# Gated cross-attention and FFN on one core: queries projected from an x turned on the host, with the layer norm folded into the weights and the rotation tables

## The chip, the cores and the metric

The kernel runs on one core of one Trainium2 chip. The metric is device microseconds of one execution. Every time in this document comes from such an execution or from its hardware trace.

## The reference

Sixteen batches of 256 tokens with 512 channels attend to 16 contexts of 256 tokens with 256 channels (32 heads of 16), and an FFN follows. Cut to what matters here:

```
def _layernorm(x, axis=-1, eps=1e-05):
    m = jnp.mean(x, axis=axis, keepdims=True)
    v = jnp.var(x, axis=axis, keepdims=True)
    return (x - m) / jnp.sqrt(v + eps)
...
q = (x @ Wq).reshape(b, n, N_HEADS, HEAD_DIM)
k, v = jnp.split(ctx @ Wkv, 2, axis=-1)
...
q = apply_axial_rope(q, pos_map)
k = apply_axial_rope(k, ctx_pos_map)
logits = jnp.einsum('bqhd,bkhd->bhqk', q, k) * scale
w = jax.nn.softmax(logits, axis=-1)
attn = jnp.einsum('bhqk,bkhd->bqhd', w, v)
...
x = x + jnp.tanh(g_xattn[0]) * _L0_xattn_ref(_layernorm(x), ctx_1024, pos, pos, Wq, Wkv, Wout, bout)
x = x + jnp.tanh(g_ffn[0]) * _L0_ffn_ref(_layernorm(x), gate_w, up_w, down_w, expert_weight, ln_gamma, ln_beta)
```

The rotation turns pairs of query and of key channels by angles that depend on the token's position: out = x1·cos − x2·sin and x1·sin + x2·cos.

## The kernel before

Each engine runs its own instruction stream, written out by hand; semaphores join them. The attention half is a software pipeline. Iteration i has 16 steps (s = 0 to 15), one for each pair of heads. In each step TensorE (PE) does first `logits_a` of one batch (stk and stq into the PSUM tile pA), then `logits_b` of another (into pB), then in some steps `times_v` (probabilities times values into pO, one group of four heads at a time), and last the jobs that the table `SCHEDULE` names for the step: K0, K1, Q0, Q1 project a tile of 128 tokens; kT0 to qT1 turn rotated tiles; V, O and m are values, output projection and the maxima turned; b0 and b1 spread the softmax denominators. X0 and X1 turn a normalised tile of x, so that Q0 and Q1 can take it as their stationary operand. `LAG` says how many batches ahead of i a job works: two for all of the query and key side, so they run in iterations 0 to 13.

VectorE (DVE) follows in the same steps: `maxima` (pA to mneg), then the evacuation of the jobs of the step before. pA is one tile: `logits_a` of step s+1 waits until `maxima` of step s is done. In step 5 and step 14 DVE also runs `reciprocals`: a RECIPROCAL on den, a CAST to den_hi and a TENSOR_TENSOR to den_lo, each waiting for the last.

The products are done in two float32r parts: a rounded value (hi, by ScalarE or GpSimd) and the rest (lo). For a query tile t of batch b the chain before is:

```
ln_statistics: bn_stats, bn_aggr of xin[t]          DVE
inv_std:       var+eps, then power -0.5 into rstd    POOL
ln_apply:      xn = (xin[t] - mean) * rstd           DVE, 128x512
X:             4 transposes of xn into pP            PE
evacuate X:    xnT[0] = round(pP)                    ACT, 128x512
               xnT[1] = pP - xnT[0]                  DVE, 128x512
Q:             12 products of xnT and wq_s           PE
evacuate Q:    rot_q = pP * cos, rot2 = pP' * sin    DVE, 2 x 128x512
rope_sum:      rot_q += rot2                         POOL
```

GpSimd (POOL) does these in an order of its own in each iteration: `inv_std`, `rope_sum` K0, `rest_av` (waits for ACT's rounding `round_av` of step 4), `rope_sum` Q0, two additions of gbout to xres, `rope_sum` K1, `rest_av`, `rope_sum` Q1, `inv_std`, `split_ctx`. SyncE (SP) issues all DMAs in one in-order queue. ACT takes the exponentials out of pB, evacuates hi parts and copies pO to av_s (`take_av`). Before the pipeline stands an opening (`OPENING`) that prepares batches 0 and 1; after it the FFN runs over eight blocks of 512 tokens. In iteration 15 `norm_in` and `turned` already prepare the first FFN tiles.

## Time and profile before

| | us |
|---|---|
| median of 3 runs (1580.32 to 1586.48) | 1585.53 |
| time of the profiled execution | 1587.19 |
| its span | 1585.4 |
| PE busy | 1522.9 (96%) |
| DVE busy | 982.8 (62%) |
| ACT busy | 632.4 (40%) |
| POOL busy | 337.9 (21%) |

The opening lasts to about 62 us, the attention pipeline to about 745 us, and the rest is the FFN. The span is the time from the first to the last instruction in the trace, the time adds what lies around it (1.8 us). A busy PE is not a PE at its peak, since the ends of pipelined matmuls are modelled. The granted clock, in tenths of full speed, is a row of the page.

### The profile page before, as it was taken

The page shows a single profiled execution, that of the slowest core. Times are in us where ns is not written, and L with a number is a line of the kernel's source. Part 1 is how long each engine was busy: PE and PEld are TensorE (multiplying, and loading weights), DVE is VectorE, ACT ScalarE, POOL GpSimd, SP SyncE. Part 2 cuts the span into 40 slices and gives each one's busy share as a digit, 9 for nine tenths or more (in the row PEclk, how much of TensorE's full clock was granted, in tenths as well). Part 3 has the DMA queues.
Part 4 walks back from the last instruction along what each step waited for, and adds up shares of the span by engine and source line. Part 5 has one row for each costly group of instructions (what it writes and reads, how often), then busy time and mean ns, then how long its engine had stood idle before and what let it go on. Part 6 is the DMA issues. An engine that isn't in the chain of part 4 may idle for free.

```text
span 1585.4 us, 25920 instructions
## 1 busy us (share of the span) xinstructions
PE 1522.9 (96%) x9498; PEld 1127.8 (71%) x9498; DVE 982.8 (62%) x1416; ACT 632.4 (40%) x962; POOL 337.9 (21%) x406
## 2 busy tenths in 40 slices
PE   7789999999999999978999999999999999999997
PEld 6556666666666666545787888878878878788886
DVE  7788888888888888755663535426344364353524
ACT  3265555555556565655442222222222222222221
POOL 5323233233323323211101102102010020110202
PEclk9699999999999999987999999999999999999999
DMA  6645555555565555543430101101010011010101
GB/s 171 141 97 142 132 132 134 129 144 133 130 144 129 126 126 137 121 121 97 140 100 14 47 20 47 34 1 54 27 34 28 20 47 34 14 47 20 54 0 41
DMA packets 80623, 131.11 MB, mean 83 GB/s; under 512 B 21624, under 2 KB 35064, under 8 KB 80504
## 3 DMA queue, kind: packets, MB, share of 16 engines
q1 hardware_dynamic: 80504, 129.48, 31.9%
q8 instruction: 80, 1.31, 0.3%
q14 instruction: 39, 0.32, 0.1%
HBM read 51.17 MB, written 16.78 MB: 43 GB/s over the span
## 4 chain that ended last, share of the span: by engine, by line
PE 84%; DVE 8%; issue 4%; POOL 2%; ACT 1%; DMA 0%; SPq 0%; POOLq 0%; DVEq 0%; ACTq 0%
PE pP L1111 17%; PE pT L1111 11%; PE pA L1312 11%; PE pO L1111 11%; PE pB L1312 11%; PE pO L1237 6%; PE pA L1209 6%; DVE mneg L1532 4%; PE pM L1111 3%; PE pB L1225 3%; PE pP L1118 2%; PE pM L1279 1%; PE pT L1193 1%; PE pM L1118 1%; PE pM L1185 1%
## 5 line engine op out<-in xcount | busy, mean ns | idle before, releaser
L1532 DVE TENSOR_REDUCE mneg<-pA 128x4 f32<-128x1024 f32 x250 | 305.7, 1223 | 111.9 <-PE pA L1209 109.0
L1010 ACT ACTIVATE probs<-pB 128x1024 f32<-128x1024 f32 x249 | 256.1, 1029 | 220.0 <-PE pB L1225 209.9
L1635 DVE TENSOR_TENSOR relu<-relu 128x512 f32<-128x512 f32 x128 | 88.3, 690 | 252.6 <-ACT hid L1064 252.6
L810 POOL TENSOR_SCALAR var_eps<-meanvar 128x1 f32<-128x1 f32 x96 | 34.5, 360 | 965.8 <-DVE meanvar L1414 965.6
L1312 PE MATMUL pA<-dn,hid 128*128 128x512 f32 x768 | 197.1, 392 | 1.7 <-DVE hid L1637 1.5
L1312 PE MATMUL pB<-dn,hid 128*128 128x512 f32 x768 | 195.0, 389 | 0.0
L1111 PE MATMUL pP<-fT,up 128*128 128x512 f32 x768 | 188.5, 394 | 0.0
L1111 PE MATMUL pO<-fT,up 128*128 128x512 f32 x768 | 184.9, 390 | 0.1
L1312 PEld LDWEIGHTS pA<-dn,hid 128*128 128x128 f32 x768 | 142.9, 188 | 34.4 <-DVE hid L1637 5.1
L1111 PEld LDWEIGHTS pO<-fT,up 128*128 128x128 f32 x768 | 143.9, 188 | 30.7 <-issue 0.8
L1312 PEld LDWEIGHTS pB<-dn,hid 128*128 128x128 f32 x768 | 144.2, 188 | 30.0
L1111 PEld LDWEIGHTS pP<-fT,up 128*128 128x128 f32 x768 | 142.0, 188 | 30.1
L1209 PE MATMUL pA<-stk,stq 48*128 48x256 f32 x1000 | 129.4, 338 | 28.0 <-DVE mneg L1532 25.1
L1209 PEld LDWEIGHTS pA<-stk,stq 48*128 48x128 f32 x1000 | 76.8, 190 | 103.7 <-issue 54.0
L1237 PE MATMUL pO<-probs,v 128*17 128x256 f32 x2048 | 138.8, 390 | 2.0 <-ACT probs L1010 2.0
L1057 ACT ACTIVATE relu<-pO 128x512 f32<-128x512 f32 x64 | 38.3, 598 | 241.6 <-PE pO L1111 241.6
L1057 ACT ACTIVATE relu<-pP 128x512 f32<-128x512 f32 x64 | 38.3, 598 | 193.7 <-PE pP L1111 193.7
L1225 PE MATMUL pB<-stq,stk 50*128 50x256 f32 x996 | 102.0, 283 | 0.0
L1111 PE MATMUL pT<-wo,aT_hi 128*128 128x512 f32 x256 | 98.4, 426 | 1.1 <-DVE numer L1470 0.6
L1111 PE MATMUL pT<-ex,fT 128*128 128x512 f32 x384 | 92.3, 389 | 0.0
L1637 DVE TENSOR_TENSOR hid<-relu,hid 128x512 fp32r<-128x512 f32 x128 | 88.7, 693 | 4.4
L1111 PE MATMUL pP<-wq,xnT 128*128 128x512 f32 x336 | 90.7, 405 | 0.0
(200 smaller groups left out, 1997.3 us busy)
## 6 DMA issues: line engine op xcount, KB each, us to landing
stk<-kT SPq DMA_DIRECT2D x180, 128.0 KB, 2.9
stq<-qT SPq DMA_DIRECT2D x180, 128.0 KB, 3.0
fres<-x_scratch SPq DMA_DIRECT2D x34, 256.0 KB, 2.8
xin<-x SPq DMA_DIRECT2D x32, 256.0 KB, 2.9
numer<-av_s SPq DMA_DIRECT2D x128, 64.0 KB, 2.4
xres<-x SPq DMA_DIRECT2D x32, 256.0 KB, 2.8
x_scratch<-xres SPq DMA_DIRECT2D x32, 256.0 KB, 2.1
out<-y_s SPq DMA_DIRECT2D x32, 256.0 KB, 2.0
```

Source lines behind the costliest of these rows:

```text
L810: nc.gpsimd.tensor_scalar_add(var_eps[:], meanvar[:, 1:2], EPS).then_inc(ve_made, 1)
L1010: nc.scalar.activation(probs[:, s % 4, :, :, :].rearrange("p a b s -> p a (b s)"), psum[:, :, :], ACT.Exp).then_inc(exp_done, 1)
L1057: nc.scalar.activation(relu[m % 2][:], pU[m % 2], ACT.Relu).then_inc(relu_made, 1)
L1111: last = nc.tensor.matmul(dst, lhs(a, c), rhs(w, c), start=(c == 0 and (a, w) == PASSES[0]), stop=(c == chunks_ - 1 and (a, w) == PASSES[-1]))
L1118: last = nc.tensor.transpose(dst[:, c * P:(c + 1) * P], src(c), ident[:])
L1209: last = nc.tensor.matmul(psum[:, q, t * S:(t + 1) * S], st_q[par][rows, s, t * P:(t + 1) * P], st_k[par][rows, s, :], start=True, stop=True)
L1225: last = nc.tensor.matmul(psum[:, q, t * S:(t + 1) * S], st_k[par][rows, s, t * P:(t + 1) * P], st_q[par][rows, s, :], start=True, stop=True)
L1237: last = nc.tensor.matmul(pO[32 * j:32 * j + HD + 1, 0:S], v_s[par][:, t, 4 * g + j, :], probs[:, (2 * g + j // 2) % 4, j % 2, t, :], star ...
L1312: last = nc.tensor.matmul(acc[u], hid[m % 2][x_][:, u * P:(u + 1) * P], dn_s[w][:, m, :], start=(m == 0 and k == 0), stop=(m == MC - 1 and ...
L1532: nc.vector.tensor_reduce(mneg[par][:, :, 2 * u:2 * u + 2].rearrange("p t q -> p q t"), psum[:, :, :].rearrange("p q (t k) -> p q t k", t= ...
L1635: nc.vector.tensor_tensor(r[:], r[:], r[:], ALU.mult).then_inc(sq_made, 1)
L1637: nc.vector.tensor_tensor(hid[m % 2][1][:], r[:], hid[m % 2][0][:].bitcast(F32), ALU.subtract).then_inc(hid_lo, 1)
```

## The change

- The host passes x a second time, each 128-token tile turned (`xT`). `load_xT` brings it into the tile xn, and `split_x` on POOL makes xnT[0] and xnT[1] from it, for every batch from 2 on. X0 and X1 leave the schedule, and with them ln_apply and both evacuations in the loop (the opening keeps them for batches 0 and 1).
- The mean is taken out of the weights: in the opening PE multiplies wq by a matrix of 1/512 (eight products into pO), ACT copies the result, SP loads wq's four chunks again into the probs tile, and POOL subtracts and splits them anew (`centre_weights`, twelve instructions of 128x512). ACT waits for two chunks before the first exponential of iteration 0 and for all four in its step 3; PE waits for them before Q0 of batch 2.
- The factor 1/std goes into the tables: `scale_tables` on DVE multiplies the tile's 32 columns of cos_t and of sin_t by rstd, in step 3 for tile 0 and in step 8 for tile 1, after the key's rotation has used them and a step ahead of the query's.
- `times_v` and `take_av` of group 1 move from step 4 to 5, of group 3 from 8 to 9.
- At the pipeline's end `norm_in` stands one step earlier, and POOL's first inv_std for the FFN ahead of rest_av.

```
@@ SCHEDULE
-    0: ("X0",),
+    0: (),
-    5: ("kT0", "X1"),
+    5: ("kT0",),
+VALUES = {2: 0, 5: 1, 6: 2, 9: 3, 10: 4, 12: 5, 14: 6}
@@ planned work at the end
-        norm_at = {(i, s - 1): u for (i, s), u in tile_at.items()}
+        norm_at = {(i, s - 2): u for (i, s), u in tile_at.items()}
@@ SyncE
             def load_x(b, t):
...
-                    sp.wait_ge(xn_made, n - 1)
+                    sp.wait_ge(xn_made if n <= TT * 2 + 1 else st_made, n - 1)
...
+            def load_xT(b, t):
+                if (b, t) == (2, 0):
+                    sp.wait_ge(*done_of("X1", 1))
+                else:
+                    sp.wait_ge(xT_split, 2 * (split_no(b, t) - 1))
+                alone(sp)
+                sp.dma_start(xn[:], xT[b * TT + t]).then_inc(xT_in, INC)
...
+            load_xT(2, 0)
+            sp.wait_ge(*done_of("kT1", 1))
+            sp.wait_ge(w_lo, KC - 2 + CC)
+            for c in range(KC):
+                sp.dma_start(raw_again[c], chunks[CC + c][0]).then_inc(w_again[c], INC)
@@ GpSimd
+            def split_x(b, t):
+                n = split_no(b, t)
+                used, of = ("Q0", b) if t else ("Q1", b - 1)
+                pool.wait_ge(*done_of(used, of))
+                pool.wait_ge(xT_in, INC * n)
+                alone(pool)
+                xv = xn[:].rearrange("p (c s) -> p c s", c=KC)
+                nc.gpsimd.tensor_copy(xnT[0][:], xv).then_inc(xT_split, 1)
+                pool.wait_ge(xT_split, 2 * n - 1)
+                nc.gpsimd.tensor_tensor(xnT[1][:], xv, xnT[0][:].bitcast(F32), ALU.subtract).then_inc(xT_split, 1)
...
                 if prepares:
                     rope_sum(b2, "Q0")
+                    split_x(b2, 1)
@@ ScalarE
-                    if s % 2 == 0 and s and within(i):
-                        take_av(i, s // 2 - 1)
+                    if s in VALUES and within(i):
+                        take_av(i, VALUES[s])
...
+            act.wait_ge(col_done, 1)
+            nc.scalar.copy(col_mean, pO[:, :]).then_inc(col_made, 1)
             later_setup()
@@ TensorE, end of the opening
+                for c in range(KC):
+                    for w in range(2):
+                        last = nc.tensor.matmul(pO[:, :], mean_w[:], wq_s[w][:, c, :],
+                                                start=(c == 0 and w == 0), stop=(c == KC - 1 and w == 1))
@@ VectorE
+            def scale_tables(b, t):
+                n = TT * b + t
+                dve.wait_ge(rstd_made, n + 1)
+                dve.wait_ge(*taken_of(f"K{t}", b))
+                alone(dve)
+                for side in (cos_t, sin_t):
+                    own = side[:, n, :, :, :].rearrange("p w k l -> p (w k l)")
+                    nc.vector.tensor_scalar(own, own, rstds[t][:, 0:1], None, ALU.mult).then_inc(scaled, 1)
...
-                    elif s == 3 and within(i + 2) and not first:
-                        ln_apply(i + 2, 1)
+                    elif s in (3, 8) and within(i + 2) and not first:
+                        scale_tables(i + 2, 0 if s == 3 else 1)
...
-                    elif s == 15 and within(i + 3):
-                        ln_apply(i + 3, 0)
```

On DVE, from step 3 to step 6 of one iteration of the loop, before:

```order
255 L1470 TENSOR_TENSOR numer<-pT,numer 128x512
256 L1418 TENSOR_SCALAR xn<-xin,meanvar,rstd 128x512
257 L1532 TENSOR_REDUCE mneg<-pA 128x2x2
258 L1460 TENSOR_TENSOR low<-pM,low 16x256
259 L1454 TENSOR_TENSOR rot_q<-pP,cos_t 128x512
```

The same place on DVE after the change:

```order
243 L1552 TENSOR_TENSOR numer<-pT,numer 128x512
244 L1607 TENSOR_SCALAR cos_t<-cos_t,rstd 128x32
245 L1607 TENSOR_SCALAR sin_t<-sin_t,rstd 128x32
246 L1623 TENSOR_REDUCE mneg<-pA 128x2x2
247 L1542 TENSOR_TENSOR low<-pM,low 16x256
248 L1536 TENSOR_TENSOR rot_q<-pP,cos_t 128x512
```

One 128x512 instruction on xn became two of 128x32 on the tables; two more stand behind the rotation of K1 in step 8.

On POOL, one iteration before (rot_k and rot_q are the rope sums, the sum over rest is rest_av):

```order
107 L817 TENSOR_TENSOR rot_k<-rot_k,rot 128x512
108 L802 TENSOR_TENSOR rest<-numer,aT_hi 128x512
109 L817 TENSOR_TENSOR rot_q<-rot_q,rot 128x512
110 L849 TENSOR_TENSOR xres<-xres,gbout 128x512 x2
111 L817 TENSOR_TENSOR rot_k<-rot_k,rot 128x512
112 L802 TENSOR_TENSOR rest<-numer,aT_hi 128x512
113 L817 TENSOR_TENSOR rot_q<-rot_q,rot 128x512
```

The same iteration on POOL after the change:

```order
142 L852 TENSOR_TENSOR rot_k<-rot_k,rot 128x512
143 L837 TENSOR_TENSOR rest<-numer,aT_hi 128x512
144 L852 TENSOR_TENSOR rot_q<-rot_q,rot 128x512
145 L861 CAST xnT<-xn 128x512
146 L863 TENSOR_TENSOR xnT<-xn,xnT 128x512
147 L909 TENSOR_TENSOR xres<-xres,gbout 128x512 x2
148 L852 TENSOR_TENSOR rot_k<-rot_k,rot 128x512
149 L837 TENSOR_TENSOR rest<-numer,aT_hi 128x512
150 L852 TENSOR_TENSOR rot_q<-rot_q,rot 128x512
151 L861 CAST xnT<-xn 128x512
152 L863 TENSOR_TENSOR xnT<-xn,xnT 128x512
```

A CAST and a TENSOR_TENSOR of 128x512 follow each of the two query sums.

On PE, steps 4 and 5 and the head of step 6 before:

```order
344 L1209 MATMUL pA<-stk,stq 128x256 x4
345 L1225 MATMUL pB<-stq,stk 128x256 x4
346 L1237 MATMUL pO<-probs,v 17x256 x8
347 L1111 MATMUL pT<-wv,ctx 128x512 x6
348 L1209 MATMUL pA<-stk,stq 128x256 x4
349 L1225 MATMUL pB<-stq,stk 128x256 x4
350 L1118 MATMUL pM<-ident,rot_k 128x128 x4
351 L1118 MATMUL pP<-ident,xn 128x128 x4
352 L1209 MATMUL pA<-stk,stq 128x256 x4
```

The same place on PE after:

```order
336 L1289 MATMUL pA<-stk,stq 128x256 x4
337 L1305 MATMUL pB<-stq,stk 128x256 x4
338 L1181 MATMUL pT<-wv,ctx 128x512 x6
339 L1289 MATMUL pA<-stk,stq 128x256 x4
340 L1305 MATMUL pB<-stq,stk 128x256 x4
341 L1317 MATMUL pO<-probs,v 17x256 x8
342 L1188 MATMUL pM<-ident,rot_k 128x128 x4
343 L1289 MATMUL pA<-stk,stq 128x256 x4
```

The values' products moved from step 4 to step 5 and the transposes of xn left it.

## Rows read from the trace of the kernel before

**Rows 1.** The page, granted clock in 40 slices of the span.

```profile
PEclk9699999999999999987999999999999999999999
```

**Rows 2.** Groups of instructions by form, 200 to 700 us: count | busy, mean ns.

```profile
L1118 PE MATMUL pP<-ident,xn 128*128 128x128 f32 x84 | 13.2, 279 | 0.0
...
L825 POOL CAST ctx<-ctx_raw 128x512 fp32r<-128x512 f32 x10 | 6.1, 611 | 0.0
```

**Rows 3.** Timeline (start, us, engine), PE, logits_a of steps 0 and 1.

```profile
318.77 0.51 PE L1209 MATMUL pA<-stk,stq 48*128 48x256 f32 x4
...
321.03 0.51 PE L1209 MATMUL pA<-stk,stq 48*128 48x256 f32 x4
```

**Rows 4.** Timeline, PE, logits_a of steps 4, 5, 7, 8, 10; values in 4.

```profile
286.44 0.50 PE L1209 MATMUL pA<-stk,stq 48*128 48x256 f32 x4
...
287.11 1.06 PE L1237 MATMUL pO<-probs,v 128*17 128x256 f32 x16
...
289.69 0.50 PE L1209 MATMUL pA<-stk,stq 48*128 48x256 f32 x4
...
293.58 0.50 PE L1209 MATMUL pA<-stk,stq 48*128 48x256 f32 x4 [0.33 <-DVE mneg L1532]
...
297.19 0.50 PE L1209 MATMUL pA<-stk,stq 48*128 48x256 f32 x4
...
302.69 0.51 PE L1209 MATMUL pA<-stk,stq 48*128 48x256 f32 x4 [0.41 <-DVE mneg L1532]
```

**Rows 5.** Timeline, DVE, from Q0's rotation to the maxima of step 6.

```profile
289.06 0.67 DVE L1457 TENSOR_TENSOR rot<-pP,sin_t 128x512 f32<-128x512 f32 x1
290.24 1.23 DVE L1532 TENSOR_REDUCE mneg<-pA 128x4 f32<-128x1024 f32 x1 [0.51 <-PE pA L1209]
...
291.95 0.19 DVE L1480 CAST den_hi<-den 64x64 fp32r<-64x64 f32 x1
292.17 0.22 DVE L1482 TENSOR_TENSOR den_lo<-den,den_hi 64x64 fp32r<-64x64 f32 x1
292.31 1.21 DVE L1532 TENSOR_REDUCE mneg<-pA 128x4 f32<-128x1024 f32 x1
```

**Rows 6.** Timeline, ACT, the exponential of step 4 and the rounding behind it.

```profile
287.23 1.02 ACT L1010 ACTIVATE probs<-pB 128x1024 f32<-128x1024 f32 x1 [1.11 <-PE pB L1225]
...
288.61 0.62 ACT L981 CAST aT_hi<-numer 128x512 fp32r<-128x512 f32 x1
```

**Rows 7.** Timeline, POOL, the same stretch.

```profile
290.55 1.27 POOL L817 TENSOR_TENSOR rot_q<-rot_q,rot 128x512 f32<-128x512 f32 x1
...
300.24 1.27 POOL L817 TENSOR_TENSOR rot_k<-rot_k,rot 128x512 f32<-128x512 f32 x1 [3.51 <-DVE rot L1457]
```

**Rows 8.** Timeline, DVE, normalisations beside POOL work; K1's rotation.

```profile
17.58 1.65 DVE L1418 TENSOR_SCALAR xn<-xin,meanvar,rstd 128x512 f32<-128x512 f32 x1
...
23.46 0.55 DVE L1418 TENSOR_SCALAR xn<-xin,meanvar,rstd 128x512 f32<-128x512 f32 x1 [0.63 <-POOL rstd L812]
...
299.48 0.68 DVE L1457 TENSOR_TENSOR rot<-pM,sin_t 128x512 f32<-128x512 f32 x1
...
318.20 1.12 DVE L1418 TENSOR_SCALAR xn<-xin,meanvar,rstd 128x512 f32<-128x512 f32 x1
```

**Rows 9.** Timeline, POOL, beside them.

```profile
17.67 1.28 POOL L817 TENSOR_TENSOR rot_k<-rot_k,rot 128x512 f32<-128x512 f32 x1 [0.20 <-DVE rot L1457]
...
317.75 1.29 POOL L827 TENSOR_TENSOR ctx<-ctx_raw,ctx 128x512 fp32r<-128x512 f32 x1
```

**Rows 10.** Timeline, PE, end of the opening.

```profile
41.20 1.53 PE L1111 MATMUL pP<-wv,ctx 128*128 128x512 f32 x6
42.57 0.60 PE L1118 MATMUL pB<-ident,rot_q 128*128 128x128 f32 x4
```

**Rows 11.** Timeline, ACT, end of the opening: the load of Tanh's table.

```profile
43.87 1.28 ACT L932 ACT_TABLE_LOAD   x1
```

**Rows 12.** Timeline, PE, iteration 15: the first FFN tile is turned.

```profile
715.40 0.90 PE L1118 MATMUL pP<-ident,fx 128*128 128x128 f32 x3 [3.44 <-DVE fx L1418]
```

More of the change, by code:

```diff
@@ L223, in sb1, with under @@
             return first.enter_context(nc.sbuf_tensor(name, shape, dt))
-        def under(name, shape):
-            with nc.sbuf_tensor(name, shape, F32) as tile:
+        def under(name, shape, dt=F32):
+            with nc.sbuf_tensor(name, shape, dt) as tile:
                 return tile
@@ L260, in flamingo_gated @@
         rest_0 = [sb1("rest_00", [P, 2, S], F32R)]
+        mean_w = under("mean_w", [P, P], F32R)
+        col_mean = under("col_mean", [P, 2, D])
         aT_hi = sb1("aT_hi", [P, KC, S], F32R)
@@ L292, in flamingo_gated, with split_no @@
         rot_k1 = raw1[0]
+        raw_again = [raw1[k] for k in (0, 1, 6, 7)]
+        def split_no(b, t):
+            return TT * (b - 2) + t + 1
         def rot_of(name, b):
@@ L375, in flamingo_gated @@
         xn_made = sem("xn_made")
+        xT_in = sem("xT_in")
+        xT_split = sem("xT_split")
+        mean_w_made = sem("mean_w_made")
+        w_again = [sem(f"w_again{c}") for c in range(KC)]
+        col_done = sem("col_done")
+        col_made = sem("col_made")
+        centred = sem("centred")
+        scaled = sem("scaled")
         p_done = sem("p_done")
@@ L614, in iteration @@
                     load_stack(b1, (par + 1) % 2, 1, "k")
+                if within(b2):
+                    load_xT(b2, 1)
                 if ending:
@@ L833, in iteration @@
                 if prepares:
-                    inv_std(b2 * TT + 2)
+                    inv_std(b2 * TT + 2, 1)
                     rope_sum(b2, "K0")
+                if isinstance(i, int) and i == B - 1:
+                    inv_std(NT + 1)
                 if within(bt):
@@ L839, in iteration @@
                     rope_sum(b2, "Q0")
+                    split_x(b2, 1)
                 ending = isinstance(i, int) and i == B - 1
                 if ending:
-                    for u in range(2):
-                        inv_std(NT + u + 1)
+                    inv_std(NT + 2)
                 if within(bt):
@@ L856, in iteration @@
                 if within(i + 3):
+                    if i < 0:
+                        split_ctx(i + 3, (par + 1) % 2)
+                    split_x(i + 3, 0)
+                    if i < 0:
+                        centre_weights()
                     inv_std((i + 3) * TT + 1)
-                    split_ctx(i + 3, (par + 1) % 2)
+                    if i >= 0:
+                        split_ctx(i + 3, (par + 1) % 2)
                 if ending:
@@ L872, in _ @@
             split_weights(CC + 2, EARLY)
-            inv_std(2)
+            inv_std(2, 1)
             rope_sum(0, "K0")
@@ L879, in _ @@
             rope_sum(0, "Q1")
-            inv_std(4)
+            inv_std(4, 1)
             rope_sum(1, "K0")
@@ L1002, in iteration @@
                             act.wait_ge(w_lo, W1 - CC - 2)
+                        if i == 0 and s in (0, 3):
+                            act.wait_ge(centred, 3 * 2 if s == 0 else 3 * KC)
                         if isinstance(i, int) and i == 0 and s in (1, 2):
@@ L1157, in opening @@
                         job(value, -1, -1)
+                pe.wait_ge(mean_w_made, 1)
+                for c in range(KC):
+                    for w in range(2):
+                        last = nc.tensor.matmul(pO[:, :], mean_w[:], wq_s[w][:, c, :],
+                                                start=(c == 0 and w == 0), stop=(c == KC - 1 and w == 1))
+                last.then_inc(col_done, 1)
                 pe.wait_ge(o_taken, len(OPENING))
@@ L1165, in compute @@
                 elif name[0] == "Q":
+                    if not opened(name, b):
+                        if (b, t) == (2, 0) and half != 1:
+                            pe.wait_ge(centred, 3 * KC)
+                        pe.wait_ge(xT_split, 2 * split_no(b, t))
                     last = product(psum, lambda a, c: xnT[a][:, c, :], lambda w, c: wq_s[w][:, c, :], KC, half)
@@ L1260, in iteration @@
                         logits_b(i, par % 2, s)
-                    if s % 2 == 0 and s and within(i):
-                        times_v(i, par % 2, s // 2 - 1)
+                    if s in VALUES and within(i):
+                        times_v(i, par % 2, VALUES[s])
                     elif s == 0 and within(i - 1):
@@ L1452, in view @@
                         return a.rearrange("p (h w e) -> p h w e", w=2, e=ANG * PAIR)
+                    if name[0] == "Q" and not opened(name, b):
+                        dve.wait_ge(scaled, 2 * split_no(b, t))
                     nc.vector.tensor_tensor(view(rot_of(name, b)), xv, table(cos_t), ALU.mult)
```

26 lines of the change are left out of this document (20 added, 6 removed), and 4 rows, old and new, of tables (BANK, LAG).

## The prediction

> **What bounds the kernel now.** I read the clock row first: TensorE is at full clock nearly everywhere but in the opening and around 680 to 730 us [rows 1], so what counts in the loop is the order of work. Then I read the timelines of PE, DVE, ACT and POOL over one iteration; the loop repeats to 0.05 us, from the row at 302.69 in iteration 5 to the one 42.92 later. The gap between two logits_a is the length of a step. A step can't be shorter than a chain through the one tile pA: the maxima start 0.55 behind the start of logits_a (289.69 to 290.24), and the next logits_a starts 1.27 behind theirs (292.31 to 293.58): 1.82 us [rows 4, 5]. Where PE has more than that to do, it sets the step. Steps 4, 5 and 6 take 7.14 together (286.44 to 293.58), steps 8 and 9 take 5.50 (297.19 to 302.69), step 0 takes 2.26 (318.77 to 321.03) [rows 3, 4]. Two of these ends are PE idle time for DVE's maxima, 0.33 and 0.41 [rows 4].
>
> **What the change takes away.** *Step 0* loses X0, four transposes of 279 ns that overlap and fill about 0.6 us [rows 2]. It falls from 2.26 to the floor of 1.82: −0.44. DVE can follow, for the normalisation that stood between the maxima of steps 15 and 0 and ended at 319.32 is gone [rows 8].
>
> *Steps 4 to 6.* Values of group 1 (1.06, of which 0.07 under the next product, [rows 4]) go from step 4 into step 5, where X1 was. logits_a of step 5 comes 1.0 earlier, so DVE no longer idles the 0.51 ahead of its maxima (row at 290.24). They then start 0.60 behind the sine product at 289.06, at 289.66 rather than 290.24: everything behind moves up by 0.58, den_hi from 291.95 to 291.37 and the maxima of step 6 from 292.31 to 291.73 [rows 5]. If nothing else stood in the way, that would be −0.58.
>
> *Steps 8 and 9.* Group 3 goes from 8 to 9. Step 9 was at the floor of 1.82 with 0.67 for its logits and 0.6 for kT1, 1.27 of work; with the group's 1.0 it is 2.26, and step 8 falls by 1.0 from 3.67 to 2.68. 4.94 for the two: −0.56 if nothing else stands in the way.
>
> Together −1.58 an iteration, times 14 iterations: −22 us. That is the whole of what the change can give in the loop.
>
> **What it adds, and where it stands.** POOL gets two casts (0.61, [rows 2]) and two subtractions (1.29, like the row at 317.75, [rows 9]) an iteration, 3.8 us. POOL is busy for 21% of the span, so in time alone this is free. The question is the port. The normalisation on DVE takes 0.55 us alone (row at 23.46). At 318.20 it began inside a POOL instruction that ran from 317.75 to 319.04, and it ended at 319.32, 0.28 behind POOL's end. At 17.58 it began 0.09 ahead of POOL's at 17.67, which ended at 18.95, and still it ended at 19.23, again 0.28 behind [rows 8, 9]. All 28 normalisations of the loop that met such a POOL instruction end 0.27 to 0.29 behind it. So such a DVE instruction (SBUF in and out) does not run beside a 128x512 one of POOL, and a lead of 0.09 does not save it.
>
> The Trainium skill, SBUF — State Buffer, Who interferes with whom, calls this an exclusive lock: copy, cast and tensor_scalar in a 2-port mode, and instructions with two SBUF inputs, block against GpSimd for the whole instruction, and whoever issues first has it. The row at 17.58 differs from that last clause: DVE issued first and lost. By the clause alone den_hi below would have a 50:50 chance at the tie, and the loop would end near the second rival.
>
> Three places of the new order meet this.
>
> (a) *Step 3*, first pair of scale instructions: they start while POOL sums K0, as the normalisation did, and are free again with its end. Nothing changes, 0.
>
> (b) *Step 8*, second pair: directly behind the sine product of K1 (299.48 to 300.16). POOL's sum of K1 starts at 300.24, off the same semaphore, and ends at 301.51 [rows 7, 8]. The scaling starts within 0.1 of it, so by the row at 17.58 it loses, and ends about 0.15 behind 301.51. Behind it wait the maxima of step 9, which nobody held before. They start at 301.65 instead of at about 300.4, so logits_a of step 10 starts at 301.65 + 1.27 = 302.92, against 302.69 now: +0.23 instead of −0.56.
>
> (c) *Step 5*, den_hi and den_lo of the reciprocals. ACT's rounding of step 4 loses the copy of pO ahead of it and starts behind the exponential: 288.25 instead of 288.61 [rows 6]. So rest_av and the sum of Q0 come 0.36 to 0.45 earlier: the sum starts at 290.1 to 290.2 and ends at 291.4 [rows 7]. The new cast starts right there, 291.4 to 292.0, and the subtraction from 292.1 to 293.4. DVE reaches den_hi at 291.37, with no lead worth the name. It waits for the cast's end; den_lo starts behind it at about the time of the subtraction, waits for that too, and ends at about 293.45. The maxima of step 6 then start at 293.37 instead of 292.31: +1.06 for the three steps instead of −0.58. PE waits there 1.8 us.
>
> The price of the 128x32 scaling and of den_hi (64x64, 0.19) beside POOL is not in the trace. From below it is nothing (they are too short to be caught), from above the wait for the whole of POOL's instruction. I take the upper one, since the rows are of the same operations and differ only in length.
>
> **The opening.** PE has eight products more behind 43.17 (42.57 + 0.60). Six take 1.37 (41.20 to 42.57), so eight take 1.8 [rows 10]. ACT copies the result (0.6) and only then loads Tanh's table, at 45.7 instead of 43.87 [rows 11]; the first maxima wait for what Tanh feeds. +1.9. Five more loads of 256 KB stand ahead of two stack loads in SP's queue, which are needed only later; bounds 0 and +3, taken at 0. The twelve centring instructions (eight of 1.29 and four of 0.61, 12.8 us on POOL) are hidden behind DVE's sixteen first maxima (over 1.1 us each) and are needed whole only in step 2 of iteration 0; without that cover they would cost up to as much again. In the loop, two xT loads an iteration find SP's queue with room, and split_x of Q1 has 1.5 us in hand before PE asks.
>
> **The end.** In iteration 15 PE idles 3.44 us for the first FFN tile [rows 12]; inv_std ahead of rest_av and the earlier normalisation save 0 to 3 of it, while in iteration 14 the values of group 3 now stand behind b1, which waits for a DMA: +1.0, the price of one group [rows 4]. Taken together −1 (bounds −9, if the clock stays up as well, and +3).
>
> **The sum.** Step 0: 14 × −0.44 = −6.2. Steps 4 to 6: 13 × 1.06 = +13.8 and −0.6 for iteration 0, which has no reciprocals there. Steps 8 and 9: 14 × 0.23 = +3.2. Opening +1.9, end −1. Sum +11.1 on the profiled execution's 1587.2: 1598.3. That execution lies 1.7 above the median of the runs, so for a median I say 1597.
>
> **The rivals.**
>
> *The short instructions aren't held at all.* Then (b) and (c) are free: 14 × −1.58 + 1.9 − 1 = −21.2, so 1564. For it: no small DVE instruction is seen held in this trace. Against it: nothing in the rows makes the wait depend on length. Chance 0.2. It decides if den_lo keeps its 0.22 us while POOL splits.
>
> *The race in step 5 goes the other way.* If den_hi gets in ahead of the cast (it needs a lead of more than 0.09), den_lo waits only for the cast, until 292.1, and the maxima of step 6 start near 292.1, −0.2 an iteration: −6.2 − 2.8 − 0.6 + 3.2 + 0.9 = −5.5, so 1580. If POOL comes 0.6 or more later, both are through before it: 14 × −0.58 for the steps 4 to 6, sum −10.2, 1575. Chance 0.25 for the two, of it 0.15 for the first.
>
> *The scaling of step 8 gets through but den_lo doesn't.* 14 × −0.56 in place of +3.2: sum +0.1, 1586. Chance 0.08.
>
> *The centring comes late.* If POOL reaches it late or is slowed, PE's Q0 of batch 2 waits at half clock, +5 to +10 on top. Chance 0.02 by itself.
>
> **How the numbers follow.** Forecast 0.45, with a range of its own from 1591 to 1604 (opening and end bounds). A measurement of this kernel tells about 0.5%, 8 us, from no change: 1577.6 and 1593.5 are the borders. Faster: 0.2 + 0.10 and a part of the first race case, 0.32. Same: the rest of that and 0.08, some of the forecast's low end, 0.22. Slower 0.46. The range 1564 to 1604 reaches to the unheld case, since both signs carry much of the chance.
>
> **What the profile after would show.** PE idle in front of logits_a of step 7 of 1.5 us or more, released by maxima; den_lo near 1.2 us instead of 0.22 in step 5 but not in step 14; the second scaling pair lasting until just behind POOL's K1 sum; period of the loop near 43.8 instead of 42.92. Right in the good case would be a period near 41.4 and den_lo at 0.22. I would be wrong by timing alone if POOL's cast starts 0.1 later than I put it, and wrong in kind if den_lo runs through POOL's subtraction.

## The result and the profile after

| | before | after |
|---|---|---|
| median, us | 1584.78 (4 runs, 1580.32 to 1586.48) | 1574.31 (4 runs, 1573.93 to 1576.58) |
| span of the profiled execution | 1585.4 | 1572.8 |
| period of the loop (mean of 12 iterations) | 42.92 | 42.49 |
| steps 4 to 6 (start of logits_a of 4 to that of 7) | 7.14 | 6.97 |
| steps 8 and 9 | 5.50 | 5.70 |
| step 0 | 2.26 | 1.83 |

The ratio is 0.9939, with a 95% interval of 0.9922 to 0.9956: faster by 0.6%, where the forecast was 1597, slower.

The profiled execution of before lies 2.4 us above the median of its runs, that of after 0.3: the spans differ by 12.6, the medians by 10.5. All sums by stages below are of spans.

The page of after, two of its lines: the engines' busy times and the clock row.

```profile
PE 1504.4 (96%) x9394; PEld 1114.7 (71%) x9394; DVE 971.5 (62%) x1416; ACT 619.1 (39%) x935; POOL 403.9 (26%) x475
PEclk9799999999999999999999999999999999999999
```

The clock row is 9 from the third slice on, where before had 8 and 7 near the end of the attention half [rows 1]. POOL is busy for 404 us instead of 338.

The starts of logits_a in the timeline of PE, one iteration of after (start, duration, tile, and the idle time ahead with its releaser in brackets):

```profile
327.85 0.50 PE L1289 MATMUL pA<-stk,stq 48*128 48x256 f32 x4
330.11 0.50 PE L1289 MATMUL pA<-stk,stq 48*128 48x256 f32 x4
332.35 0.51 PE L1289 MATMUL pA<-stk,stq 48*128 48x256 f32 x4
334.82 0.50 PE L1289 MATMUL pA<-stk,stq 48*128 48x256 f32 x4 [0.73 <-DVE mneg L1623]
...
338.45 0.50 PE L1289 MATMUL pA<-stk,stq 48*128 48x256 f32 x4
341.14 0.50 PE L1289 MATMUL pA<-stk,stq 48*128 48x256 f32 x4
344.15 0.50 PE L1289 MATMUL pA<-stk,stq 48*128 48x256 f32 x4 [0.60 <-DVE mneg L1623]
```

DVE and then POOL in the same stretch, a fence for each:

```profile
331.07 1.20 DVE L1623 TENSOR_REDUCE mneg<-pA 128x4 f32<-128x1024 f32 x1
332.20 0.53 DVE L1560 RECIPROCAL den<-den 64x64 f32<-64x64 f32 x1
332.77 0.61 DVE L1562 CAST den_hi<-den 64x64 fp32r<-64x64 f32 x1
333.41 0.22 DVE L1564 TENSOR_TENSOR den_lo<-den,den_hi 64x64 fp32r<-64x64 f32 x1
333.55 1.21 DVE L1623 TENSOR_REDUCE mneg<-pA 128x4 f32<-128x1024 f32 x1
...
340.74 0.68 DVE L1539 TENSOR_TENSOR rot<-pM,sin_t 128x512 f32<-128x512 f32 x1
341.56 1.25 DVE L1607 TENSOR_SCALAR cos_t<-cos_t,rstd 128x32 f32<-128x32 f32 x1
...
342.88 1.21 DVE L1623 TENSOR_REDUCE mneg<-pA 128x4 f32<-128x1024 f32 x1
```

```profile
331.50 1.27 POOL L852 TENSOR_TENSOR rot_q<-rot_q,rot 128x512 f32<-128x512 f32 x1
332.72 0.61 POOL L861 CAST xnT<-xn 128x512 fp32r<-128x512 f32 x1
333.41 1.35 POOL L863 TENSOR_TENSOR xnT<-xn,xnT 128x512 fp32r<-128x512 f32 x1
...
341.50 1.28 POOL L852 TENSOR_TENSOR rot_k<-rot_k,rot 128x512 f32<-128x512 f32 x1 [3.35 <-DVE rot L1539]
```

Put beside [rows 5, 7], with logits_a of step 4 at 327.85 where it was at 286.44 (an offset of 41.41): the forecast's maxima of step 5 (289.66) stand at 331.07 and its den_hi (291.37) at 332.77, both within 0.01. The cast was to start at 291.4 and started at 332.72, 0.09 ahead of it; den_hi is held as I said, 0.61 instead of 0.19. Then both engines start in the same hundredth, 333.41. I had den_lo wait out the subtraction. It takes its 0.22, and the subtraction takes 1.35 instead of 1.28. That is so in all 13 iterations that have the pair (the two starts within 0.003 of each other). Not every VectorE instruction between SBUF tiles is held: the RECIPROCAL at 332.20 starts 0.70 into POOL's sum and takes 0.53, what it takes in step 14, where POOL does nothing. In step 8 the scaling at 341.56, 0.06 behind POOL's sum, lasts 1.25 and delays the maxima to 342.88, as forecast.

The sum by stages, from the starts of V0 in step 14 (before and after): at 41.20 and 40.79 in the opening, 100.64 and 101.79 in iteration 0, 658.31 and 653.79 in iteration 13.

| us against before | forecast | measured |
|---|---|---|
| opening and iteration 0 | 1.9 − 0.44 − 0.58 + 0.23 = +1.1 | +1.15 |
| 13 iterations | 13 × 0.85 = +11.1 | −4.52 − 1.15 = −5.67 |
| end (iteration 14 on) | −1 | −12.6 + 4.52 = −8.1 |
| span | +11.1 | −12.6 |

So two terms were off: the steps 4 to 6, by 13 × 1.23 = 16.0 us, and the end, by 7.1 us. That the first row agrees to 0.05 is in part luck: in single executions of the eight kernels that share this opening and this iteration 0 (after, e1, e8 to e10, e13 to e15), its V0 starts anywhere from 101.8 to 103.0.

Stretches of the end in before, and then in after. Each row has the window, its length, the busy time (and number of instructions) of PE, PEld, DVE, ACT and POOL, then the granted clock, the busy share of the DMA engines and GB/s:

```profile
681.00:686.00 5.00, 2.75 (x18) 2.26 (x18) 1.82 (x2) 1.29 (x2) 0.97 (x1) 0.50 0.63 137
...
717.00:722.00 5.00, 4.11 (x40) 1.80 (x40) 2.17 (x4) 3.89 (x6) 0.00 (x0) 0.50 0.51 138
722.00:727.00 5.00, 4.01 (x26) 2.26 (x18) 2.21 (x3) 1.59 (x3) 3.42 (x4) 0.50 0.27 44
```

```profile
676.00:681.00 5.00, 5.00 (x38) 2.96 (x42) 2.30 (x3) 1.96 (x4) 1.60 (x3) 0.51 0.69 150
681.00:686.00 5.00, 5.00 (x40) 3.18 (x34) 1.98 (x2) 2.38 (x3) 1.17 (x1) 1.00 0.35 56
...
712.00:717.00 5.00, 5.00 (x30) 2.66 (x30) 2.07 (x4) 2.09 (x4) 1.45 (x2) 0.50 0.58 98
717.00:722.00 5.00, 5.00 (x34) 2.98 (x33) 1.15 (x2) 3.26 (x5) 2.04 (x3) 0.85 0.40 64
722.00:727.00 5.00, 4.79 (x44) 2.90 (x46) 2.22 (x5) 3.33 (x5) 0.79 (x2) 1.00 0.44 153
```

Before, the clock is at 0.5 (the level of 1.2 GHz) over whole stretches of 10 and 17 us; in after it is back at 1.0 from 681 and 719 on. Summed over windows of 1 us between 640 and 760, before stands at half clock for 27.3 us and after for 17.1 (here with a third stretch, from 749 on).

### The profile page after: what moved, and what is told of

It is laid out like the page before. It is cut to its first block, busy times and chain, and to the rows that moved or that the text cites. A ratio compares the mean times of both kernels' runs of the same rounds, so it can differ in the third digit from the quotient of the medians.

```text
span 1572.8 us, 25873 instructions
## 1 busy us (share of the span) xinstructions
PE 1504.4 (96%) x9394; PEld 1114.7 (71%) x9394; DVE 971.5 (62%) x1416; ACT 619.1 (39%) x935; POOL 403.9 (26%) x475
## 4 chain that ended last, share of the span: by engine, by line
PE 54%; DVE 2%; issue 1%; ACT 1%; POOL 0%; DMA 0%; SPq 0%; POOLq 0%; DVEq 0%; ACTq 0%
PE pP L1181 11%; PE pA L1392 11%; PE pO L1181 11%; PE pB L1392 11%; PE pT L1181 5%; PE pO L1317 1%; PE pM L1359 1%; PE pM L1188 1%; PE pA L1289 1%; DVE mneg L1623 0%; DVE relu L1724 0%; ACT hid L1134 0%; DVE hid L1726 0%; PE pB L1305 0%; ACT relu L1127 0%
```

## The experiments

The first theory after the result (A): the shared port goes to whoever asks first and for the whole instruction, and at equal start to den_lo. Its rival (B): den_lo, with two inputs and 64x64, is of a kind that POOL doesn't hold. Periods below are means of 12 iterations, from the V0 of iteration 1 to that of 13.

### e1: something ahead of den_lo

```diff
                 dve.wait_ge(rc_made, 3 * n + 2)
+                nc.vector.memset(idle[:], 0.0)
                 nc.vector.tensor_tensor(den_lo[:, :], d, den_hi[:, :].bitcast(F32), ALU.subtract).then_inc(rc_made, 1)
```

> The changed kernel with one more small DVE instruction (a memset of 64x16) between den_hi and den_lo, so that den_lo starts shortly after POOL's subtraction of split_x instead of in the same 0.01 us (both 333.41 in the trace of the changed kernel). Theory A, the port goes to whoever is first and den_lo only won a tie: den_lo is now held until the subtraction ends, about 1.35 instead of 0.22, the maxima of step 6 start 1.1 to 1.3 later, the steps 4 to 6 take 8.1 to 8.2 instead of 6.97, and the kernel takes 13 x 1.2 = 15.6 us more, 1590. Theory B, den_lo is of a kind (two inputs, 64x64) that the subtraction does not hold: den_lo keeps 0.22, the steps take 0.1 more, and the kernel 1575 to 1576.

Measured: 1575.51, ratio to before 0.9946 (0.9928 to 0.9964), period 42.50. DVE, then POOL:

```profile
333.54 0.20 DVE L1566 TENSOR_TENSOR den_lo<-den,den_hi 64x64 fp32r<-64x64 f32 x1
333.54 0.07 DVE L1565 MEMSET idle<- 64x16 f32 x1
```

```profile
333.51 1.35 POOL L864 TENSOR_TENSOR xnT<-xn,xnT 128x512 fp32r<-128x512 f32 x1
```

That is the outcome that was put down for B. But the memset took no time of its own: den_lo moved to only 0.03 behind the subtraction's start, so B was hardly put to the test, and I did not count it. It adds one point: den_lo 0.03 behind is still not held, so A can't mean the recorded start to the last hundredth.

### e10: another cast ahead of den_hi

```diff
                 dve.wait_ge(rc_made, 3 * n + 1)
+                nc.vector.tensor_copy(spare[:, :], d)
                 nc.vector.tensor_copy(den_hi[:, :], d).then_inc(rc_made, 1)
```

> The changed kernel with one more cast of den (64x64, into a spare tile) ahead of den_hi, so that den_hi, a cast, and no longer den_lo starts together with POOL's subtraction in step 5. Theory B, the kind decides: den_hi is held for the subtraction's whole length, takes about 1.4 instead of 0.61, the steps 4 to 6 rise from 6.97 to about 8.3, 13 x 1.3 = +17, 1591. Theory A, the tie goes to DVE: den_hi takes 0.2, den_lo behind it is held instead: also +1.3. The two differ in which of the two instructions is long; that neither is long (+0.2 an iteration, 1577) would be a third, only the cast of POOL holds anything.

Measured: 1600.4, ratio 1.0111 (1.0083 to 1.0139), period 44.39. DVE and then POOL in one iteration:

```profile
342.57 0.61 DVE L1563 CAST spare<-den 64x64 fp32r<-64x64 f32 x1
343.11 0.18 DVE L1564 CAST den_hi<-den 64x64 fp32r<-64x64 f32 x1
343.32 1.25 DVE L1566 TENSOR_TENSOR den_lo<-den,den_hi 64x64 fp32r<-64x64 f32 x1
```

```profile
343.22 1.28 POOL L864 TENSOR_TENSOR xnT<-xn,xnT 128x512 fp32r<-128x512 f32 x1
```

It came out in a way that I had not set up: the spare cast was held by POOL's cast, den_hi got in 0.11 ahead of the subtraction, and den_lo, now 0.10 behind it, was held to its end: 1.25 instead of 0.22. B falls. A stands, with its tie a few hundredths wide. The steps 4 to 6 take 2.26 + 2.24 + 3.60 = 8.10 in that iteration, +0.96 against the kernel before: this is the case that I had forecast at +1.06.

But the period rose by 1.90 against after, and not by 1.13. What is behind the wait shows it. PE, one iteration later, and the windows behind that wait (columns as above):

```profile
389.38 0.64 PE L1290 MATMUL pA<-stk,stq 48*128 48x256 f32 x4 [1.87 <-DVE mneg L1625]
```

```profile
391.00:393.00 2.00, 2.00 (x6) 1.61 (x5) 0.28 (x1) 0.50 (x1) 1.20 (x1) 0.50 0.91 199
393.00:395.00 2.00, 2.00 (x15) 1.42 (x14) 0.00 (x0) 0.00 (x0) 0.00 (x0) 1.00 0.91 200
```

PE had idled 1.87 us; then the granted clock fell to 0.50, and step 7 took 5.14 instead of 3.61. The same idle time stands in all 13 iterations with reciprocals in step 5, and the fall follows in six of them (every second one from the third on). So the hold cost 1.13 us an iteration against after, and six times 1.53 on top. The forecast had PE wait "1.8 us" there and did not price the clock.

### e9: probes where nobody waits

```diff
+                nc.vector.tensor_tensor(probe[0:64, 288:352], gbout[0:64, 0:64], gbout[0:64, 64:128], ALU.subtract)
+                nc.vector.tensor_tensor(probe[:, 0:256], gbout[:, 0:256], gbout[:, 256:512], ALU.subtract)
+                nc.vector.tensor_copy(probe[64:128, 288:352], gbout[64:128, 64:128])
+                nc.vector.tensor_scalar(probe[:, 256:288], gbout[:, 0:32], meanvar[:, 0:1], None, ALU.mult)
```

> The changed kernel with four more DVE instructions in step 7, which nobody waits for: DVE idles 2.4 us there while POOL adds gbout to xres (two instructions of 1.27, 335.61 to 338.15 in the trace of the changed kernel). In order: a subtraction of two 64x64 inputs in SBUF, one of two 128x256 inputs, a copy 64x64, a tensor_scalar 128x32. In iteration 0 POOL has no such additions in that step, so the same four show there what they take alone. Theory B, the kind decides: both two-input instructions take inside POOL's additions what they take alone (about 0.2 and 0.4), the copy or the tensor_scalar is held to the end of the addition it meets. Theory A, whoever is first has the port: the first subtraction, which starts 0.9 into an addition, is held to its end near 336.9 or to that of the second, 338.15. The period stays at 42.49 by both.

One run, 1575.32, period 42.56. The first three in iteration 0, where POOL does nothing; then the same three in a later iteration, and POOL there:

```profile
85.25 0.21 DVE L1611 TENSOR_TENSOR probe<-gbout 64x64 f32<-64x64 f32 x1
85.38 0.41 DVE L1612 TENSOR_TENSOR probe<-gbout 128x256 f32<-128x256 f32 x1
85.81 0.19 DVE L1613 COPY probe<-gbout 64x64 f32<-64x64 f32 x1
```

```profile
337.61 0.43 DVE L1611 TENSOR_TENSOR probe<-gbout 64x64 f32<-64x64 f32 x1
337.97 0.41 DVE L1612 TENSOR_TENSOR probe<-gbout 128x256 f32<-128x256 f32 x1
338.39 1.19 DVE L1613 COPY probe<-gbout 64x64 f32<-64x64 f32 x1
```

```profile
336.67 2.86 POOL L910 TENSOR_TENSOR xres<-xres,gbout 128x512 f32<-128x512 f32 x2 [0.80 <-DMA xres<-x]
```

The small subtraction began 0.94 into POOL's first addition and was held to its end (336.67 + 1.27 = 337.94): 0.43 instead of 0.21. The next slipped in between the two additions and took the 0.41 that it takes alone, while the two additions took 2.86 instead of 2.54. The copy was held for the second: 1.19 instead of 0.19. Two inputs, copy, small or larger: each is held or gets in by when it asks. The Trainium skill, SBUF — State Buffer, Who interferes with whom, says of copies and other instructions in a 2-port mode "Whoever issues first gets the shared pair for the whole instruction", and that an instruction with two SBUF inputs contends with a GpSimd instruction that reads SBUF. The trace agrees for both kinds: 1.25 (e10) and 0.43 for two inputs, 1.19 for the copy.

### e13, e14, e15: three forms at the same tie

What stayed open is [rows 8, 9]: a normalisation that began 0.09 ahead of POOL and was held. Each of these puts one instruction between den_hi and den_lo, so that it starts with POOL's subtraction (within 0.01 of it).

```diff
e13:
+                nc.vector.tensor_scalar(spare[0:64, 0:64], gbout[0:64, 0:64], meanvar[0:64, 0:1], None, ALU.mult)
e14:
+                nc.vector.tensor_tensor(spare[0:64, 0:64], gbout[0:64, 0:64], gbout[0:64, 64:128], ALU.subtract)
e15:
+                nc.vector.tensor_scalar(spare[:, :], gbout[:, 0:352], meanvar[:, 0:1], meanvar[:, 1:2], ALU.subtract, ALU.mult)
```

> The changed kernel with a tensor_scalar of 64x64 with one scalar operand from SBUF between den_hi and den_lo, so that it meets POOL's subtraction at equal start. If reading its scalar makes such an instruction ask for the port late, it is held: about 1.3 instead of 0.2, and the steps 4 to 6 rise by 1.3. If the kind makes no difference, it wins as den_lo did, den_lo behind it is the one held (1.2), and the steps rise by as much: the two differ in which instruction is long.

> The same with a subtraction of two 64x64 inputs in that place: it should win the tie as den_lo did (0.2), and den_lo, now 0.15 to 0.2 behind POOL's start, should be held for about 1.2. If it is held itself, the tie in the changed kernel was won for a reason of den_lo alone.

> The same with a tensor_scalar of 128x352 with two scalar operands, the form of the normalisation, in that place. If it is held (about 1.5 instead of 0.4) while e13's is not, size or the second scalar decides; if both are held, the scalar operand; if neither, the row of the normalisation (0.09 ahead and held) has another cause.

One run each: 1613.54, 1606.09, 1614.74, with periods of 45.48, 44.96 and 45.47. Step 5 on DVE and POOL in e13, and then in e14:

```profile
351.57 1.32 DVE L1565 TENSOR_SCALAR spare<-gbout,meanvar 64x64 f32<-64x64 f32 x1
```

```profile
351.57 1.27 POOL L864 TENSOR_TENSOR xnT<-xn,xnT 128x512 fp32r<-128x512 f32 x1
```

```profile
347.45 0.22 DVE L1565 TENSOR_TENSOR spare<-gbout 64x64 f32<-64x64 f32 x1
347.59 1.28 DVE L1566 TENSOR_TENSOR den_lo<-den,den_hi 64x64 fp32r<-64x64 f32 x1
```

```profile
347.44 1.35 POOL L864 TENSOR_TENSOR xnT<-xn,xnT 128x512 fp32r<-128x512 f32 x1
```

At equal start the small tensor_scalar with a scalar operand from SBUF loses (1.32 instead of the 0.25 that it takes in step 14) and the subtraction keeps its 1.27; e15's large one loses too (1.47 instead of 0.46). The small two-input instruction wins (0.22), the subtraction takes 1.35, and den_lo, 0.15 behind POOL's start, is held for 1.28. So at equal start the form decides: a tensor_scalar with a scalar operand loses where a two-input instruction wins, at either size.

For the row of the normalisation, 0.09 ahead and held, that is not the whole answer, for a lead helps some forms. The first scaling of iteration 0 (one scalar operand) starts 0.03 to 0.04 ahead of POOL's sum in seven of the traces. It is held in four of them, as in after, here with POOL's row, and gets in in three, as in e16, the row behind it:

```profile
74.96 1.37 DVE L1607 TENSOR_SCALAR cos_t<-cos_t,rstd 128x32 f32<-128x32 f32 x1
74.99 1.29 POOL L852 TENSOR_TENSOR rot_k<-rot_k,rot 128x512 f32<-128x512 f32 x1
```

```profile
75.11 0.23 DVE L1607 TENSOR_SCALAR cos_t<-cos_t,rstd 128x32 f32<-128x32 f32 x1
```

In e16 POOL's sum begins at 75.15 and takes 1.35. With 0.08 of lead the second scaling of the pair gets in ahead of POOL's cast, as in e4:

```profile
322.15 0.23 DVE L1607 TENSOR_SCALAR sin_t<-sin_t,rstd 128x32 f32<-128x32 f32 x1
322.23 0.62 POOL L861 CAST xnT<-xn 128x512 fp32r<-128x512 f32 x1
```

The normalisation (two scalar operands, 128x512) with the same lead is held in all 16 traces that have it. Whether its second scalar, its size or the instruction that it meets makes that difference no run separates; nor does any have a tensor_scalar without a scalar from SBUF, or a cast, at equal start with a subtraction. Why a scalar operand makes an instruction late (it may be read before the instruction asks for the port) is argued, not shown.

### e2, e3, e4, e12: out of each other's way

```diff
 e2, e4, e12: POOL's iteration
                     rope_sum(b2, "K0")
+                    split_x(b2, 1)
...
                     rope_sum(b2, "Q0")
-                    split_x(b2, 1)
 e3, e4, e12: DVE's iteration, scaling of tile 1
+                    if s == 9 and within(i + 2) and not first:
+                        scale_tables(i + 2, 1)
                     for name in names_at(i, s - 1) if s else names_at(i - 1, STEPS - 1):
...
-                    elif s in (3, 8) and within(i + 2) and not first:
-                        scale_tables(i + 2, 0 if s == 3 else 1)
+                    elif s == 3 and within(i + 2) and not first:
+                        scale_tables(i + 2, 0)
```

> The changed kernel with POOL's split_x of tile 1 moved from behind the sum of Q0 to behind the sum of K0, where POOL idles for 2.17 us ahead of rest_av. Theory: den_hi was held by the cast (0.61 instead of 0.19), so it falls to 0.19 and the steps 4 to 6 from 6.97 to about 6.55, the -0.58 of the unhindered case: 14 x -0.41 = -5.8, 1568.5. Rival: the wait of DVE isn't what ends last there (PE or the next hold takes over), then under 2 us change. Second rival: the split there holds up the second pair member or another DVE instruction of steps 3 and 4, then the same or slower.

> The changed kernel with the second pair of scale instructions moved from behind the rotation of K1 in step 8 (where POOL's sum of K1 holds the first for 1.25) to behind the maxima of step 9, ahead of the rotation of Q1. Theory: steps 8 and 9 fall from 5.70 to about 4.94, -0.76 an iteration, 14 x -0.76 = -10.6, 1563.7. Rival: the 0.6 of the pair goes in front of the rotation of Q1, and the steps 10 to 12, where DVE has three evacuations in a row, take it back: -0.2 an iteration or less, 1571 to 1574.

> Both moves together: split_x of tile 1 ahead of rest_av, the second scale pair in step 9. If the two holds are independent the gains add: -0.41 and -0.76 an iteration, 14 x -1.17 = -16.4, 1558. If the loop has another bound (PE's own work, or SP's queue), less than the sum.

| | median | ratio to before (95%) | period |
|---|---|---|---|
| e2 | 1570.91 | 0.9912 (0.9894 to 0.9930) | 42.12 |
| e3 | 1565.37 | 0.9873 (0.9854 to 0.9893) | 41.83 |
| e4 | 1561.26 | 0.9854 (0.9833 to 0.9874) | 41.47 |

DVE in e4, the reciprocals of step 5 and the first of the pair in step 9:

```profile
326.87 0.19 DVE L1562 CAST den_hi<-den 64x64 fp32r<-64x64 f32 x1
327.09 0.22 DVE L1564 TENSOR_TENSOR den_lo<-den,den_hi 64x64 fp32r<-64x64 f32 x1
...
336.49 0.23 DVE L1607 TENSOR_SCALAR cos_t<-cos_t,rstd 128x32 f32<-128x32 f32 x1
```

None of the three is held any more: 0.19, 0.22, 0.23. The steps 4 to 6 take 6.54 in e4, the unhindered 7.14 − 0.58 of the forecast within 0.02. That is so in 11 of the 13 iterations; in the other two the transfer of xT lands late, the cast, the subtraction and the sum behind it come later, and den_hi is held by that sum (0.38 and 0.92). Steps 8 and 9 take 5.03, not 4.94, in e3 and e4. The two moves are worth 0.37 and 0.66 an iteration, and they add (1.02 in e4). e4 beats both kernels.

e12 is e4 with ACT's two Tanh ahead of the copy of the column means:

```diff
+            later_setup()
             act.wait_ge(col_done, 1)
             nc.scalar.copy(col_mean, pO[:, :]).then_inc(col_made, 1)
-            later_setup()
```

> The kernel with both moves (split_x ahead of rest_av, scaling in step 9), and in the opening ACT does its two Tanh ahead of the copy of the column means, so that the table load does not stand behind PE's eight products. Theory: the first maxima come 1.3 to 1.9 earlier, and the centring starts 0.5 later without anybody waiting for it: 1561.3 - 1.5 = 1559.8. Rival: the centring ends what the exponentials wait for in iteration 0, and the time is the same.

Measured 1560.68, ratio 0.9852 (0.9827 to 0.9877). The first maxima start at 45.74 instead of 47.17 in e4, but V0 of iteration 0 at 100.74 instead of 101.22. Of 1.4 us some 0.9 is given back by then. What takes it was not isolated, the start of that V0 differs by as much between single executions of kernels with one opening, and in the time e12 can't be told from e4.

### e5 to e8, e11, e16: which part brings what

e5 and e16 put the values back, in after and in e4; e6 moves them in the kernel before; e7 and e8 do or undo the end's part; e11 is e6 and e7 together.

```diff
 e5, e16 (e6 the other way round, in the kernel before)
-VALUES = {2: 0, 5: 1, 6: 2, 9: 3, 10: 4, 12: 5, 14: 6}
+VALUES = {2: 0, 4: 1, 6: 2, 8: 3, 10: 4, 12: 5, 14: 6}
 e7, e11 (e8 the other way round, in the kernel after)
-        norm_at = {(i, s - 1): u for (i, s), u in tile_at.items()}
+        norm_at = {(i, s - 2): u for (i, s), u in tile_at.items()}
...
+                if isinstance(i, int) and i == B - 1:
+                    inv_std(NT + 1)
                 if within(bt):
                     rest_av(bt, 0)
```

> The changed kernel with groups 1 and 3 of the values back in steps 4 and 8. Theory: group 1's move is what lets DVE start the maxima of step 5 0.58 earlier; without it the reciprocals come 0.58 later, the cast 0.36 later, so the steps 4 to 6 take about 7.4 instead of 6.97. Group 3's move bought nothing in the changed kernel, because the held scaling (until 342.73) already sets the maxima of step 9 there: steps 8 and 9 stay at 5.70. Together +0.45 an iteration, 13 x 0.45 = +5.9, 1580. Rival: both moves count, +1.0 an iteration, 1587; or neither, 1574.

> The kernel before with only the move of groups 1 and 3 to steps 5 and 9. Theory: steps 8 and 9 fall from 5.50 to 4.94 since no scaling is held there; steps 4 to 6 fall only by 0.2, for with X1 still in step 5 PE has 1.0 + 0.6 + 0.6 + 0.67 there and becomes the limit. Together -0.73 an iteration, 14 x -0.73 = -10, 1576: as much as the whole change. Rival: the values stood where they cost least, and PE's order makes it the same or slower, 1585 or more.

> The kernel before with only the end's part: norm_in one step earlier and POOL's first inv_std for the FFN ahead of rest_av. Theory: the idle time of 3.44 ahead of the first FFN tile falls to near 0 and with it the stretch at half clock behind it (715 to 732): -5, 1581. Rival: the wait only moves to another step of iteration 15 and the clock still falls, 0 to -2.

> The changed kernel with the end's part undone (norm_in in its old step, the first inv_std behind the sum of Q0 and the split). Theory: iteration 15 takes back about 5 us of its gain: 1579. Rival: the end's gain of 8.2 comes from elsewhere (the clock in iteration 14, fewer transposes and evacuations), then 1574 to 1576.

> The kernel before with the values' move and the end's part together, so all of the change but the queries from the host-turned x with their scaling. Theory: the values' -11.4 and a part of the end's -4.8 (both shorten the same stretch at half clock): 1568 to 1570, faster than the changed kernel by 4 to 6, so that the queries' part costs 4 to 6 as it is written. Rival: the end's part adds nothing here, 1573.

> Both moves (split_x ahead of rest_av, scaling in step 9), with groups 1 and 3 of the values back in steps 4 and 8. Theory: the steps 4 to 6 take 6.54 + 0.58 = 7.12, the steps 8 and 9 3.67 + 1.82 = 5.49 instead of 5.03, so the period is 41.40 + 1.04 = 42.44 and the time about 1575: with no hold, the move of group 3 is worth 0.46 an iteration, while it was worth nothing in the changed kernel. Rival: DVE or ACT now limits those steps and the values' place matters less, 1567 to 1570.

Period, end and half are each from one execution. "End" is the span less the start of V0 in iteration 13; "half" is the time at half clock between 640 and 760, summed as above. "Queries" is the x turned on the host with its scaling, as the change places it, or with e4's two moves.

| | parts | median | ratio to before (95%) | period | end | half |
|---|---|---|---|---|---|---|
| before | none | 1584.78 | 1 | 42.92 | 927.1 | 27.3 |
| e7 | end | 1579.53 | 0.9965 (0.9944 to 0.9985) | 42.93 | 921.2 | 23.6 |
| e6 | values | 1572.90 | 0.9932 (0.9911 to 0.9952) | 42.09 | 923.8 | 23.9 |
| e11 | values, end | 1567.09 | 0.9892 (0.9867 to 0.9918) | 42.09 | 918.9 | 13.7 |
| e5 | queries, end | 1582.13 | 0.9985 (0.9970 to 0.9999) | 42.95 | 921.0 | 23.9 |
| e16 | queries moved, end | 1582.65 | 0.9990 (0.9977 to 1.0003) | 42.95 | 920.4 | 23.9 |
| e8 | queries, values | 1578.60 | 0.9969 (0.9957 to 0.9981) | 42.53 | 921.2 | 17.1 |
| after | queries, values, end | 1574.31 | 0.9939 (0.9922 to 0.9956) | 42.49 | 919.0 | 17.1 |
| e4 | queries moved, values, end | 1561.26 | 0.9854 (0.9833 to 0.9874) | 41.47 | 917.0 | 13.7 |

What follows. The values' move alone brings more in the loop (−0.83 an iteration) than the whole change (−0.43); in e6 the steps 4 to 6 take 6.77 and the steps 8 and 9 take 5.03. The queries' part, as the change places it, gives most of that back: after stands 0.47% behind e11 (0.9939 against 0.9892). In e5 the steps 8 and 9 take 5.69 with the values' group 3 in step 8, as against 5.70 in after with it in step 9: the held scaling hid that move entirely, as expected. Without the hold it is worth 0.47: in e16 the steps 8 and 9 take 5.50, in e4 5.03. e16's other expectation missed: its period is 42.95 and not 42.44, its time 1582.65 and not 1575. Steps 4 to 6 (7.14) and 8 and 9 came out as put; the rest is in the steps 10 and 11, 3.87 and 2.51 against 3.64 and 2.26 in e4, where the rotation of Q1 starts 0.35 behind logits_a of step 10 (347.56 and 347.21) and in e4 0.16 ahead (336.98 and 337.14). That this is the cause was not tested.

The end adds up less simply, since each number is of one execution. Seven kernels that have the same end but for at most one instruction beside the reciprocals (after, e1, e9, e10, e13 to e15) have from 917.7 to 920.0 there (e13 917.9 and e9 917.8, with 20.5 and 10.2 us at half clock). Against that, the end's own part brings 5.9 (e7 against before), 4.9 (e11 against e6) and 2.2 (after against e8; 4.3 in the medians). The values bring 3.3 (e6), 2.3 (e11 against e7), 2.0 (after against e5) and 3.4 (e4 against e16). The queries bring 0.2 (e5 against e7), 2.6 (e8 against e6) and −0.1 (after against e11). So the first two are gains, to about 2 us, and the queries' share is not clear of the noise.

## Why the prediction failed, point by point

- *Step 0*: −0.44 forecast, −0.43 measured. Right.
- *Steps 4 to 6*, what comes earlier: right to 0.01 on DVE, and the hold of den_hi too. **The step that failed is (c): "den_lo starts behind it at about the time of the subtraction, waits for that too."** They start together, and den_lo has the port. −0.17 an iteration instead of +1.06, 16 us of the 23.7 between forecast and result. Behind it stands the earlier sentence "a lead of 0.09 does not save it", and that the rows "are of the same operations and differ only in length". They are not: the normalisation takes its mean and rstd as scalar operands, den_lo has none, and e13 to e15 show that this form loses a tie that the other wins. The row at 17.58 was the only near-tie shown, and the forecast gave the tie no chance of its own.
- The mechanism itself was right for casts, copies, tensor_scalar and two-input instructions: between SBUF tiles they wait out POOL's, however short. It does not hold for every instruction (the RECIPROCAL above). The first rival ("aren't held at all") is refuted by den_hi's 0.61, the scaling's 1.25, and e9, e10 and e14. The sign that the forecast named for it, a den_lo of 0.22 while POOL splits, came all the same: the sign could not tell a won tie from an instruction that is never held. "The race in step 5 goes the other way" named −0.2 an iteration for a den_lo that waits only for the cast, and that is what happened (by the tie, not by den_hi getting in ahead). Its 1580 was then too high by the end's term.
- By the Trainium skill's clause on who issues first, the prediction gave an even chance to a tie of den_hi; the tie that came was den_lo's. The clause fits the rows where the starts are 0.1 or more apart. Closer than that the recorded start does not tell who issued first: a two-input instruction gets in from 0.03 behind (e1), tensor_scalar with scalar operands is held at equal start and, as a normalisation, with a lead of 0.09.
- *Steps 8 and 9*: +0.23 forecast, +0.20 measured, and by the wait that was named. e3 gives it back.
- *Opening*: right as a sum (+1.1 and +1.15), closer than single executions agree with each other. The table load moved from 43.87 to 45.23 and the first maxima by 1.3, where +1.9 was forecast.
- *The end*: the term was mis-sized, −1 against −8.1, though −9 was named as a bound. The values' group behind b1 was priced as a loss of 1.0; in the table the values' move is a gain of 2.0 to 3.4 there. Behind the V0 of iteration 13 PE is busy for 897.6 us in before and for 893.5 in after, over the same 4282 matmuls. So about 4.2 of the 8.1 is work that ran faster, as less of it fell at half clock (17.1 us instead of 27.3), and 3.9 is less idle time. e7 shows that the earlier normalisation is worth 5.9 with nothing else changed, 4.1 of it less idle time: the 3.44 ahead of the first FFN tile goes, and a wait of 2.73 comes a little later. The clock was not tested alone, and the two columns do not run strictly together (e8 has after's 17.1 and 2.2 us more).
- Had step 5 gone as forecast, the result would have been slower than the forecast's 1597: e10 and e14 took 1600 and 1606, since the clock falls behind PE's wait in some iterations.

## What to carry to other kernels

When a change puts work on GpSimd, list for each new instruction what VectorE does between SBUF tiles at that moment, to a tenth of a microsecond, and move one of the two out of the other's way; here two such moves turned 0.6% into 1.5%. The maxima, which read PSUM, were not held (1.21 at 333.55, beside POOL's subtraction), and so are a place to put it under. Where two engines meet in the trace within 0.1 us, the outcome is a case of its own with its own chance, and a row of another form of instruction doesn't decide it. Measure the parts of a change apart as well as together: one part was hidden by another's wait, and the values' move alone did as much as the whole.
